# A transformer layer with mixture of experts on one core: levels spread by DMA in the tables, and two row tiles of the shared experts placed behind the expert slots

## What is computed

```python
levels = clip-scan over tokens (+1 for one of three opening tokens, -1 for a closing one, within 0..31)
h = level_emb[levels] * 0.15                      # 2048 rows of 256, but only 32 different ones
h = h + attention_with_relative_positions(layernorm(h))   # 16 heads of 16, 8 batches of 256
u = layernorm(h)
X = u + attention(rmsnorm(u)) @ wo
h2 = rmsnorm(X)
combine = softmax over the 2 largest of softmax(h2 @ router_w)      # 8 experts, 2 per row
moe = swiglu(h2, shared) + sum over experts of combine * swiglu(h2, expert)
out = h + X + moe
```

## Time and profile before

| | us |
|---|---|
| median of 3 runs | 792.87 (789.66 to 793.83) |
| profiled execution | 789.15 |
| its span | 787.3 |

### The profile page before, as it was taken

The page is one execution under the profiler, slowest core; times in us unless marked ns, Lnnn a source line. Parts: engine busy times, 40 slices in busy tenths (PEclk is TensorE's granted clock), DMA queues, the critical chain, the costliest instruction groups (busy, mean ns, idle before and its releaser), DMA issues. The chain is left out here.

```text
span 787.3 us, 19021 instructions
## 1 busy us (share of the span) xinstructions
PE 739.9 (94%) x7221; PEld 561.6 (71%) x7222; DVE 459.9 (58%) x1105; ACT 367.1 (47%) x608; POOL 195.1 (25%) x300
## 2 busy tenths in 40 slices
PE   3899999999999998999997989999999999999994
PEld 1377777777767886455554864555899999999993
DVE  7777777777636564999982865512334444443441
ACT  4677777767634444366764212201233333333330
POOL 5410000000003433333230540265132222323232
PEclk9999999999999999999999999999999999999997
DMA  4400000000011345444464900022432323233231
GB/s 165 175 2 2 2 3 2 2 2 2 3 48 41 104 138 159 130 122 123 126 244 138 366 26 16 29 87 79 157 50 44 54 43 51 47 47 49 45 48 20
DMA packets 70545, 58.97 MB, mean 75 GB/s; under 512 B 7552, under 2 KB 62152, under 8 KB 70480
## 3 DMA queue, kind: packets, MB, share of 16 engines
q1 hardware_dynamic: 62048, 47.61, 19.7%
q0 software_dynamic: 7152, 9.38, 7.3%
q10 hardware_dynamic: 1280, 1.08, 0.4%
HBM read 35.02 MB, written 22.95 MB: 74 GB/s over the span
## 5 line engine op out<-in xcount | busy, mean ns | idle before, releaser
L1488 POOL DMA_INDIRECT out<-ex_Y,ex_to x39 | 60.6, 1554 | 166.1 <-DVE ex_Y L1763 163.1
L652 ACT ACTIVATE la_PT<-ps 128x512 f32<-128x512 f32 x128 | 69.5, 594 | 46.5 <-PE ps L553 46.1
L1214 DVE TENSOR_REDUCE fa_m<-ps 128x2 bf16<-128x512 f32 x128 | 84.2, 683 | 6.7 <-PE ps L1083 5.5
L1717 DVE TENSOR_TENSOR ex_hT<-ps,ex_sl 128x512 f32<-128x512 f32 x39 | 27.0, 692 | 98.9 <-PE ps L1554 98.9
L1184 ACT ACTIVATE fa_PT<-ps 128x1024 f32<-128x1024 f32 x64 | 65.5, 1024 | 39.5 <-PE ps L1098 39.4
L1561 PE MATMUL ps<-WD,ex_hT 128*128 x312 | 74.0, 380 | 1.6 <-DVE ex_Y L1763 0.9
L1554 PEld LDWEIGHTS ps<-ex_xT,V 128*128 128x128 f32 x640 | 74.5, 192 | 1.1 <-ACT ex_xT L1607 0.2
L1554 PE MATMUL ps<-ex_xT,V 128*128 128x128 f32 x640 | 74.8, 275 | 0.0
L1554 PEld LDWEIGHTS ps<-ex_xT,XS 128*128 128x128 f32 x608 | 70.8, 192 | 0.9
L1554 PE MATMUL ps<-ex_xT,XS 128*128 128x128 f32 x608 | 71.0, 275 | 0.0
L671 DVE TENSOR_TENSOR la_SM<-ps,la_SA 128x512 bf16<-128x512 f32 x64 | 44.3, 692 | 37.7 <-ACT la_SA L634 19.1
(11 more groups left out here) (262 smaller groups left out, 1442.1 us busy)
## 6 DMA issues: line engine op xcount, KB each, us to landing
QK<-qk_parts SPq DMA_DIRECT2D x192, 64.0 KB, 2.3
qk_parts<-pj_parts SPq DMA_DIRECT2D x16, 384.0 KB, 2.8
expert_in<-zfill SPq DMA_DIRECT2D x1, 5070.0 KB, 16.1
ex_XR<-expert_in SPq DMA_DIRECT2D x39, 130.0 KB, 2.1
WG<-in_e_gate SPq DMA_DIRECT2D x8, 512.0 KB, 6.9
WU<-in_e_up SPq DMA_DIRECT2D x8, 512.0 KB, 10.5
...
```

The source lines that it names most:

```text
L652: nc.scalar.activation(PT[:, n // 2 % 2, jh, n % 2], ps[:, 2 * (n % 2) + jh], ACT.Exp, scale=QK_SCALE).then_inc(s_exp[jh], 1)
L1214: nc.vector.reduce_max(m[:, b % 2, grp, 2 * k:2 * k + 2], ps[:, h % 2].rearrange("p (f j) -> p f j", f=2), AX.X).then_inc(s_max, 1)
L1488: nc.gpsimd.indirect_dma_start(out=outs, out_offset=bass.IndirectOffsetOnAxis(ap=to[:, n:n + 1], axis=0), in_=Y[:, n], in_offset=None, com ...
```

## The change

In the tables: `OHX` is laid out (quad of batches, head, batch, row). The levels are stored to HBM (`g.lv`) and read back into all 128 partitions (`LEVB`, two DMAs of 256 KB), and DVE compares them there with a value per partition (`one_hot(quad)`: four comparisons of 1024 columns for `OHX`, one for `OH3`); quad 0 in the tables, quad 1 in the level attention between the six first units and the first step. The products L405 and L395, the tiles L252, L254, L351, L355 and L332 go. The copies of L666 and L630 now also reorder (h, b, i) to (b, i, h). Three of twelve slots of Q and K are written by each split step itself or copied by ACT; the identity casts go from DVE to ACT; `spin` products fill PE. POOL waits for all one-hots before its three memsets of `QK`; the load of `er` is issued earlier and the zero fill of `expert_in` after the levels.

In the experts: row tiles 14 and 15 (`HALF` = 14) leave group 3. Their residual goes to `out` at the start; after the last slots' products PE does their `up_late` and `down_late`, SP reads the two tiles back from `out` after all adds have landed, DVE adds and SP stores them. `H2T` is laid out by pairs of tiles, so that the last pair outlives the reuse of its memory. `largest` runs in two halves, the count products come before `down(0)`, and DVE does picks, shares, places, chosen and owners without products of group 1 between; the POOL waits stand at scatters 9 and 20 only.

```diff
...
-g.H2T = g.V2[:].rearrange("p t h d -> p (t h d)").rearrange("p (c t) -> p c t", c=DC)
+g.H2T = g.V2[:].rearrange("p t h d -> p (t h d)").rearrange("p (q c t) -> p q c t", c=DC, t=2 * P)
...
-        g.OHX = lo("OHX", [P, B, S, HG], BF16)
+        g.OHX = lo("OHX", [P, NQUAD, HG, BP, S], BF16)
+        g.LEVB = lo("LEVB", [P, NQUAD, BP * S], BF16)
+        g.code, g.lvl = lo("code", [P, HG], F32), lo("lvl", [L3, 1], F32)
...
+def one_hot(nc, g, quad):
+V = nc.vector
+for h in range(HG):
+last = V.tensor_scalar(g.OHX[:, quad, h].rearrange("p b i -> p (b i)"), g.LEVB[:, quad], g.code[:, h:h + 1], None, ALU.is_equal)
+last.then_inc(g.s_oh, 1)
+V.tensor_scalar(g.OH3[:, quad * BP * S:(quad + 1) * BP * S], g.LEVB[0:L3, quad], g.lvl[:, 0:1], None, ALU.is_equal).then_inc(g.s_oh, 1)
...
-    for o, i in ((sel, "sel"), (h4, "h4"), (lvl, "lvl"), (code, "code"), (iotaL, "iotaL")):
+    sp.dma_start(er[:], a["er"]).then_inc(s_in[3], 16)
+    for o, i in ((iotaL, "iotaL"), (g.lvl, "lvl"), (g.code, "code")):
...
+    sp.wait_ge(s_lv, 1)
+    sp.dma_start(g.lv.rearrange("o (b s) -> (o b) s", b=B), lev[:]).then_inc(s_lvd, 16)
+    sp.wait_ge(s_lvd, 16)
+    for q in range(NQUAD):
+        sp.dma_start(g.LEVB[:, q], g.lv[:, q * BP * S:(q + 1) * BP * S].to_broadcast([P, BP * S])).then_inc(s_lvb[q], 16)
+    sp.wait_ge(s_lvb[0], 16)
...
+    sp.wait_ge(s_lvb[1], 16)
...
+    act.wait_ge(s_in[4], 16)
+    copy(g.identB[:], g.identF[:]).then_inc(s_idb, 1)
+    nc.scalar.activation(g.negIB[:], g.identF[:], ACT.Copy, scale=-1.0).then_inc(s_idb, 1)
...
-    copy(selB[:], sel[:]).then_inc(s_keep, 1)
...
-    def one_hot(x):
-        act.wait_ge(s_ohb[1], x + 1)
-        nc.scalar.activation(sq[:, x % 2], ps[:, 2 + x % 2], ACT.Square, bias=code[:, 1:2]).then_inc(s_sq, 1)
-        act.wait_ge(s_sq, x + 1)
-        nc.scalar.activation(ohx[:, OWN[1][x]], sq[:, x % 2], ACT.Relu, bias=one[:], scale=-1.0).then_inc(s_ohx[1], 1)
...
+    for src, k, at in ((0, 0, slice(1, 4, 2)), (0, 1, slice(2, 6, 2)), (5, 0, slice(2, 3)), (5, 1, slice(1, 2))):
+        act.wait_ge(s_part, 1 if src == 0 else 2)
+        n = len(range(SLOTS)[at])
+        copy(slots[:, k, :, at], slots[:, k, :, src].unsqueeze(2).to_broadcast([P, NG, n, DK])).then_inc(s_keep, 1)
...
+    split(G, do, er[:], e1[:], e2[:], [EP[:, :, n] for n in (0, 5, 3)])
+    do(G.tensor_copy(EP[:, :, 2:6:2], EP[:, :, 0].unsqueeze(2).to_broadcast([P, 4, 2, DK])))
+    G.tensor_copy(EP[:, :, 1], EP[:, :, 5]).then_inc(s_made, 1)
...
-    V.scalar_tensor_tensor(lev4[:], lev[:].unsqueeze(2).to_broadcast([B, S, HG]), float(HG), h4[:].unsqueeze(1).to_broadcast([B, S, HG]),
...
-    for n in range(SLOTS):
-        at = slice(n * DK, (n + 1) * DK)
-        do(V.tensor_copy(g.QT[:, :, at], parts[LEFT[n]][:, 0]))
-        do(V.tensor_copy(KT[:, :, at], parts[RIGHT[n]][:, 1]))
+    do(V.tensor_copy(slots[:, :, :, 0], tab[:]), s_part)
+    do(V.tensor_tensor(r1[:], tab[:], slots[:, :, :, 0], ALU.subtract))
+    do(V.tensor_copy(slots[:, :, :, 5], r1[:]), s_part)
+    do(V.tensor_tensor(r2[:], r1[:], slots[:, :, :, 5], ALU.subtract))
+    for k, n in enumerate((4, 3)):
+        V.tensor_copy(slots[:, k, :, n], r2[:, k]).then_inc(s_part, 1)
...
-        dve.wait_ge(s_lvp, q + 1)
-        V.tensor_scalar(g.OH3[:, q * 512:(q + 1) * 512], ps[0:L3, q % 2, :], lvl[:, 0:1], None, ALU.is_equal).then_inc(s_oh, 1)
...
-        dve.wait_ge(s_ohb[0], x + 1)
-        V.tensor_scalar(ohx[:, OWN[0][x]], ps[:, x % 2], code[:, 0:1], None, ALU.is_equal).then_inc(s_ohx[0], 1)
...
+    dve.wait_ge(s_turn, 1)
+    V.tensor_copy(qkT[:, 1].rearrange("p h l -> p (h l)"), ps[0:KP, 6].bitcast(BF16)[:, 0:512]).then_inc(s_qkTc, 1)
...
+    dve.wait_ge(s_ac, 2)
+    do(V.tensor_copy(ac[:], ps[:, 0, 0:NG * L].rearrange("p (g l) -> p g l", g=NG)))
+    split(V, do, ac[:], a1[:], a2[:], [g.ACP[:, :, n * L:(n + 1) * L] for n in range(3)])
+    dve.wait_ge(s_lvb[0], 16)
+    one_hot(nc, g, 0)
+    dve.wait_ge(s_sp, 1)
+    dve.wait_ge(g.s_oh, 2)
...
-    def codes(k, x):
-        if x >= 2:
-            pe.wait_ge(s_ohx[k], x - 1)
...
-        c0 = OWN[k][x] * 512
-        mm(ps[:, 2 * k + x % 2], selB[:, c0 // (S * HG)], lev4[:].rearrange("b s h -> b (s h)")[:, c0 % (S * HG):c0 % (S * HG) + 512],
-           start=True, stop=True).then_inc(s_ohb[k], 1)
...
+    spin(nc, g, 2, 2)
+    pe.wait_ge(s_lv, 1)
...
+    spin(nc, g, 2, 3)
+    pe.wait_ge(s_part, 4)
+    pe.wait_ge(s_keep, 5)
+    for n in range(2):
+        for k in range(NG):
+            last = nc.tensor.transpose(ps[0:KP, 5 + n].bitcast(BF16)[:, k * P:(k + 1) * P], g.QKT[:, n, k], g.identB[:])
+    last.then_inc(s_turn, 1)
...
+    spin(nc, g, 2, 9)
...
+    pool.wait_ge(g.s_oh, 2 * NQUAD)
...
-        rhs = g.OHX[:, quad * BP:(quad + 1) * BP, i0:i0 + CH, :]
+        rhs = g.OHX[:, quad, :, :, i0:i0 + CH]
+        if i0 == 0 and grp == 0 and quad:
+            pe.wait_ge(g.s_oh, 2 * quad + 2)
...
+        nc.scalar.activation(AQ[:, ch % 2, grp], ps[0:L3, bank].rearrange("p (h b i) -> p b i h", b=BP, h=HG), ACT.Copy).then_inc(s_ab, 1)
...
+        nc.vector.tensor_copy(QB[:, ch % 2, grp], ps[0:KP, bank].rearrange("p (h b i) -> p b i h", b=BP, h=HG)).then_inc(s_qb, 1)
...
+    for q in range(1, NQUAD):
+        dve.wait_ge(g.s_lvb[q], 16)
+        one_hot(nc, g, q)
...
+HALF = NT - 2
+GROUPS = [slice(4 * tg, min(4 * tg + 4, HALF)) for tg in range(4)]
+LATE = (7, 4, 6, 1)
...
+    sp.dma_start(ov[:, HALF:NT], g.HS[:, HALF:NT]).then_inc(s_out, 16)
...
-        sp.dma_start(ov[:, 4 * tg:4 * tg + 4], g.HS[:, 4 * tg:4 * tg + 4]).then_inc(s_out, 16)
+        sp.dma_start(ov[:, at], g.HS[:, at]).then_inc(s_out, 16)
...
+    sp.dma_start(g.HS[:, HALF:NT], ov[:, HALF:NT]).then_inc(s_back, 16)
+    for k in range(2):
+        sp.wait_ge(s_last, k + 1)
+        sp.dma_start(ov[:, HALF + k], g.HS[:, HALF + k]).then_inc(s_out, 16)
+    sp.wait_ge(s_out, 16 * 7)
...
-            if k % 3 == 0:
-                pool.wait_ge(s_act_, min(FC + 2 + k // 3, 4 * FC))
+            if k == 9:
+                pool.wait_ge(s_act_, 2 * FC)
+            elif k == 20:
+                pool.wait_ge(s_act_, 2 * FC + 3)
...
-    pool.wait_ge(s_out, 64)
+    pool.wait_ge(s_out, 80)
...
+                    last = mm(ps[:, bk, 0:w_].rearrange("p (q t) -> p q t", t=2 * P), w[:, cc, f * P:(f + 1) * P], g.H2T[:, q, cc],
+                              start=cc == 0, stop=cc == 1)
...
+    def up_late(f):
+        if f == FC - 1:
+            pe.wait_ge(s_si, NS - 1)
+        for k, w in enumerate((SG, SU)):
+            for cc in range(DC):
+                last = mm(ps[:, LATE[f], k * 2 * P:(k + 1) * 2 * P], w[:, cc, f * P:(f + 1) * P], g.H2T[:, HALF // 2, cc],
+                          start=cc == 0, stop=cc == 1)
+        last.then_inc(s_hid, 1)
+    def down_late():
+        for k in range(2):
+            for f in range(FC):
+                if k == 0:
+                    pe.wait_ge(s_act_, 4 * FC + f + 1)
+                last = mm(ps[:, 3 - k, 0:D], hidS[:, f, k * P:(k + 1) * P], SD[:, f], start=f == 0, stop=f == FC - 1)
+            last.then_inc(s_y, 1)
...
+    up_late(0)
     down_slot(NS - 1, 0, expert_of(pe, NS - 1))
+    for f in range(1, FC):
+        up_late(f)
+    down_late()
...
-        if n == FC:
+        if n == FC - 1:
...
+    for f in range(FC):
+        n = 4 * FC + f
+        act.wait_ge(s_hid, n + 1)
+        act.wait_ge(s_act_, n - 1)
+        A(sil[:, n % 2, 0:2 * P], ps[:, LATE[f], 0:2 * P], ACT.Silu).then_inc(s_sil, 1)
...
+    largest(0)
+    V.memset(ones[:], 1.0).then_inc(s_m, 1)
+    do(V.memset(zer[:], 0.0))
+    hid(0, 512)
+    largest(1)
+    hid(1, 512)
+    picks()
+    hid(2, 512)
+    shares()
+    hid(3, 512)
+    places()
+    chosen()
+    owners()
...
+    hid_late(0)
     keep_y(NS - 1, 0, NS // 2 * 16)
+    for f in range(1, FC):
+        hid_late(f)
+    dve.wait_ge(s_back, 16)
+    for k in range(2):
+        dve.wait_ge(s_y, 4 + k + 1)
+        V.tensor_tensor(g.HS[:, HALF + k], ps[:, 3 - k, 0:D], g.HS[:, HALF + k], ALU.add).then_inc(s_last, 1)
 def kernel(**inputs):
```

More of the change, by code:

```diff
@@ L180, in tables @@
     s_in = [sem("in_" + n) for n in ("tok", "tab", "w", "er", "id", "wo", "bias", "dump", "const")]
-    s_ohb, s_ohx = ([sem("tab_" + n + k) for k in names(2)] for n in ("codes", "onehot"))
     s_dve, s_pool = sem("tab_dve"), sem("tab_pool")
-    s_lv, s_lvp, s_oh, s_sq, s_ln, s_keep, s_proj, s_sp, s_turn, s_qkTc, s_ac, s_made, s_idb, s_rs = (
-        sem("tab_" + n) for n in "levels levelsB onehot3 square norm kept proj split turned qkTc ac made idb rstd".split())
+    s_lv, s_lvd, s_ln, s_keep, s_proj, s_part, s_sp, s_turn, s_qkTc, s_ac, s_made, s_idb, s_rs = (
+        sem("tab_" + n) for n in "levels stored norm kept proj part split turned qkTc ac made idb rstd".split())
+    s_lvb = g.s_lvb = [sem("tab_spread" + n) for n in names(NQUAD)]
+    g.s_oh = sem("tab_onehot")
     with ExitStack() as c:
@@ L274, in _ @@
                 do(G.memset(half[:], -0.5))
```

(62 more changed lines are left out.)

134 lines of the change are left out of this document (39 added, 95 removed).

## The result

| | before | after |
|---|---|---|
| median, us | 793.35 (789.66 to 794.09) | 770.43 (766.41 to 772.96, 4 runs) |
| profiled execution | 789.15 | 769.5 |
| its span | 787.3 | 767.7 |

The ratio is 0.972, 95% interval 0.969 to 0.975: 22 us less, where 14.6 were forecast.

The account below looks back on a forecast made before the run. It took the tables as bound by DVE and ACT, the attention, shared experts and slots by PE, the end by a chain of waits; -11.1 + 0.9 - 10.4 + 6.0 = -14.6 us from 792.9 gave 778.3, range 772 to 787.5.

Parts of the forecast that it names:

- The end: After the last slots: late products, read back, adds, store and a 3.95 us ending would lose 6.0 us.
- The first six units: Start of the level attention: quad 1's comparisons add 2.45 us to DVE, 1.51 of it in idle time; 0.9 us lost.
- the tables' term: Tables: PE starts its next stage at 19.9 in place of 30.99 us, 11.1 us gained.
- quad 1's five comparisons: Level attention, between sixth unit and first maximum: five DVE comparisons in SBUF, 2.45 us in all.
- The slots: Expert slots: PE busy 214.56 of 215.47 us, taken as full; no gain or loss in the sum.
- the price of the comparison: Tables and level attention: a DVE comparison of 1024 bfloat16 columns in SBUF takes 0.49 us.
- rival 1: Comparison runs slower: double rate (0.78 us each) 781.2, chance 0.13; one element per step (1.32) 786.6, chance 0.12.
- the reordering copies: Level attention: DVE's copies from PSUM that now also reorder cost 0 extra.
- rival 3: Level attention: reordering copies slow, 0.55 us more per unit, 17.6 us if half is not absorbed: 795.9; chance 0.05.
- the shared experts: Shared experts: 10.4 us of PE work leave group 3, slot 0 starts 10.4 us earlier, scatters land in time.
- Rival 2: Late tiles give nothing: tail costs 10 instead of 6, or scatters come later than PE; 782.7, chance 0.12.
- The prediction's own fallback: Shared experts: if `pidx` were no earlier, 32 scatters in a row would lose 1.2 us of the gain.

Follow-up runs that it names:

- The read in the kernel before: Kernel before, with SP reading 256 KB back from the output after all adds have landed and waiting for it: 790.3 us.
- the second: Second profiled run of the unaltered kernel after: 767.6 us, ratio 0.970.
- the stores run: Kernel before, with the stores of groups 0 to 2 issued ahead of the wait for the scatters: 790.2 us, ratio 0.9972.

## Why the prediction was wrong

The direction and both mechanisms were right; the size was not. By the ratio 22 us were gained where 14.6 were forecast. The two traces account for 5.0 of that miss, and three steps make it up, less what the route lost. The rest, nearly 3 us, is what executions of one kernel differ by: with the 19.6 of the two traces the time would have been 773.3, inside the range.

**The end** is the step that failed most: "a store of 128 KB ... the ending 3.95: 793.3 in place of 787.3. 6.0 us lost". It set the 3.95 us that lay behind the last landing before as a fixed tail behind whatever comes last. The read in the kernel before cost 0.05, and after the change the span ends 767.7 - 765.05 = 2.65 behind the issue of the first of the two last stores, where 2.5 + 3.95 = 6.45 were taken; a store landed in 1.8. The end lost 2.13, so 3.9 of the miss are here. The terms ahead of it held: landing 3.77 (3.68), read back 2.70 (2.5 and 0.1), and PE ended its late products at 764.2, within 0.4 of the read's landing.

**The first six units** ("0.9 us is lost") were a gain of 0.87 beyond the tables' term: 1.8 of the miss, less 0.4 that the tables' term fell short. Two terms hold the 1.8. The units took 1.3 less (36.35 - 30.99 = 5.36 before, 24.29 - 20.26 = 4.03 after): their products ran 0.43 apart before and the first four 0.22 after. The spins, which the prediction set down as lying "where PE has nothing else to do" and costed at nothing, account for 1.05 of it by the run without them. The other 0.5 is quad 1's five comparisons, 26.26 - 24.29 = 1.97 in place of 2.45. The 0.63 us of a product at 30.99 was there to be read, beside 0.38 for one at 35.08.

**The slots** were costed at nothing, and became 1.46 shorter. The earlier trace rows held the hint: PE busy 214.56 of 215.47, 0.9 us idle that the text called full. Most of it is one stop behind 2 MB of stores: up to slot 0's down product 1.20 of the 1.46 are gained (9.52 from slot 0's start before, 8.32 after).

Against these stands the route, 1.74 us longer in the profiled execution because the clock fell; the prediction didn't treat it. This is no property of the change: with the old route and tables the clock fell there too in the read and the stores run (0.66; 0.72 and 0.60), and the profile of before happened to have none.

Right were: the tables (11.1 forecast, 10.73 in this trace, 11.80 in the second), with both loads of levels down in time, though in the first trace the comparisons began 0.6 later than forecast (17.59 for 16.95) and were 0.4 cheaper, so part of the nearness is luck; the price of the comparison, at 0.40 to 0.48 under the 0.49 (its own terms add up to 0.50) and far from 0.78, so rival 1 fell; the reordering copies at 0, so rival 3 fell; the shared experts (10.4, 10.67), with `pidx` 10 us earlier (22.0 behind the stage's start in place of 32.0). Rival 2, scatters that still decide, is false of this change but true of a kernel next to it: late choice and old waits. The prediction's own fallback (a late `pidx`, "1.2 us of the gain lost") measured 1.8. The Trainium skill, VectorE: DVE Perf Modes, section "The perf-mode tier table", gave an estimated 0.43 us for the comparison; the trace agrees, with 0.40 in a row, 0.48 alone and 0.26 ns per element, a quarter of the 1.07 of a PSUM source. Of the lock between DVE and GpSimd that the prediction took from the Trainium skill, SBUF — State Buffer, no run here is a test.
